# Macaron block on one core: feed-forward results turned in 32 by 32 squares and added onto x by a transfer; the attention numerator added up by transfers, its second product on GpSimd

## The reference

```
x = x + 0.5 * ffn(layernorm(x))        # for each of 8 experts: acc += (silu(x @ wg) * (x @ wu)) @ wd
x = x + attention(layernorm(x))        # linear attention, 16 heads of 8 channels, bias bo
x = x + 0.5 * ffn(layernorm(x))
# attention, along the 1024 positions t of a batch, per head:
#   S_t = S_{t-1} + phi(k_t) v_t^T ;  z_t = z_{t-1} + phi(k_t)
#   out_t = (phi(q_t) S_t) / (phi(q_t) . z_t + eps) ; then @ Wo.T + bo
```

## Time and profile before

| | before |
|---|---|
| device time, median of 3 runs | 2106.57 us (2105.96 to 2108.25) |
| device time of the profiled execution | 2106.5 us |
| span of the profiled execution | 2104.7 us |
| instructions | 29593 |
| PE busy | 99% |
| DVE busy | 86% |
| ACT busy | 67% |
| POOL busy | 22% |
| DMA, mean | 56 GB/s |
| granted TensorE clock | 1.0 throughout |

### The profile page before, as it was taken

The page is one execution under the profiler, slowest core; times in us unless marked ns, Lnnn a source line. Parts: engine busy times, 40 slices in busy tenths (PEclk is TensorE's granted clock), DMA queues, the critical chain, the costliest instruction groups (busy, mean ns, idle before and its releaser), DMA issues.

```text
span 2104.7 us, 29593 instructions
## 1 busy us (share of the span) xinstructions
PE 2075.6 (99%) x9716; PEld 951.7 (45%) x9716; DVE 1800.3 (86%) x3023; ACT 1416.3 (67%) x2466; POOL 459.1 (22%) x370
## 2 busy tenths in 40 slices
PE   8999999999999999999999999999999999999999
PEld 4444444444444444444444444444444444444444
DVE  8877988899889989887989888888998899877776
ACT  6777667766776686668666766677667666666665
POOL 6400122212321321122112311231132213200000
PEclk9999999999999999999999999999999999999999
DMA  7000323122222221312212232041222233100000
GB/s 206 6 11 11 91 66 76 44 68 56 71 61 67 71 56 61 82 26 61 73 45 71 56 81 63 25 96 56 67 56 71 61 76 81 31 7 10 11 11 5
DMA packets 106186, 117.84 MB, mean 56 GB/s; under 512 B 53168, under 2 KB 83504, under 8 KB 106032
## 3 DMA queue, kind: packets, MB, share of 16 engines
q1 hardware_dynamic: 106032, 115.95, 21.6%
HBM read 86.31 MB, written 17.30 MB: 49 GB/s over the span
## 4 chain that ended last, share of the span: by engine, by line
PE 86%; DVE 8%; ACT 3%; issue 3%; DMA 0%; POOL 0%; SPq 0%; ACTq 0%; DVEq 0%
PE bank L545 10%; PE bank L558 9%; PE bank L560 9%; PE bank L559 9%; PE bank L534 9%; PE bank L532 9%; PE bank L533 9%; PE bank L546 9%; PE bank L547 9%; DVE bank L834 3%; DVE h_lo L840 2%; ACT silu_sb L647 1%; DVE arena L948 1%; PE bank L617 1%; PE bank L597 1%
## 5 line engine op out<-in xcount | busy, mean ns | idle before, releaser
L647 ACT ACTIVATE silu_sb<-bank,scal 128x512 f32<-128x512 f32 x1024 | 703.2, 687 | 615.9 <-PE bank L534 611.8
L834 DVE SCALAR_TENSOR_TENSOR bank<-silu_sb,scal,bank 128x512 f32<-128x512 f32 x992 | 745.4, 751 | 283.6 <-ACT silu_sb L647 280.3
L840 DVE TENSOR_TENSOR h_lo<-bank,h_hi 128x512 f16<-128x512 f32 x992 | 674.1, 680 | 0.1
L654 ACT ACTIVATE h_hi<-bank 128x512 f16<-128x512 f32 x992 | 585.4, 590 | 6.3 <-DVE bank L834 5.1
L545 PE MATMUL bank<-xn,wu_hi 128*128 128x512 f16 x1024 | 389.0, 380 | 15.3 <-DVE h_lo L840 12.5
L532 PE MATMUL bank<-xn,wg_hi 128*128 128x512 f16 x1024 | 388.1, 379 | 2.5 <-DVE wg_lo L822 2.5
L558 PE MATMUL bank<-h_hi,wd_lo 128*128 128x512 f16 x1024 | 388.1, 379 | 0.7 <-DVE wd_lo L822 0.7
L546 PE MATMUL bank<-xn,wu_hi 128*128 128x512 f16 x1024 | 388.1, 379 | 0.0
L547 PE MATMUL bank<-xn,wu_lo 128*128 128x512 f16 x1024 | 388.1, 379 | 0.0
L534 PE MATMUL bank<-xn,wg_lo 128*128 128x512 f16 x1024 | 388.1, 379 | 0.0
L533 PE MATMUL bank<-xn,wg_hi 128*128 128x512 f16 x1024 | 388.1, 379 | 0.0
(11 more groups left out here) (126 smaller groups left out, 1343.4 us busy)
## 6 DMA issues: line engine op xcount, KB each, us to landing
arena<-rep_scratch SPq DMA_DIRECT2D x128, 512.0 KB, 7.1
rep_scratch<-arena SPq DMA_DIRECT2D x16, 512.0 KB, 2.6
x_tok<-in_L_attn_x SPq DMA_DIRECT2D x16, 256.0 KB, 5.3
term_scratch<-arena SPq DMA_DIRECT2D x8, 512.0 KB, 3.4
arena<-term_scratch SPq DMA_DIRECT2D x8, 512.0 KB, 3.2
arena<-rden_scratch SPq DMA_DIRECT2D x8, 512.0 KB, 8.6
out<-x_tok SPq DMA_DIRECT2D x16, 256.0 KB, 2.4
arena<-in_L_ffn_Wg SPq DMA_DIRECT2D x4, 512.0 KB, 8.8
```

Of the source, the lines that this page charges most:

```text
L647: act.activation(silu_sb[:, n % 3, :], gate_ps[n % NG][:, :], ACT.Silu, scale=unscale[G[group(n)]]).then_inc(sem("silu"), 1)
L654: act.activation(h_hi[:, n % NH, :], up_ps[n % NUP][:, :] if n >= NC else h_sb(n), ACT.Copy).then_inc(sem("h_hi"), 1)
L834: dve.scalar_tensor_tensor(up_ps[n % NUP][:, :] if n >= NC else h_sb(n), silu_sb[:, n % 3, :], (h_scale if n >= NC else h_first)[group(n)] ...
L840: dve.tensor_tensor(h_lo[:, n % NH, :], up_ps[n % NUP][:, :], h_hi[:, n % NH, :], ALU.subtract).then_inc(sem("h_lo"), 1)
```

## The change

What it does:

- **Segment ends** (32 of 33): VectorE turns `down_sb` in squares of 32 by 32 (`turn`, one instruction 128x512), SP writes the squares to DRAM with four transfers (`turn_out`, 64 KB each, in pieces of 128 B), and GpSimd's queue issues a transfer of 256 KB that adds them onto x (`resid`). The four TensorE transposes and the VectorE addition go. The last end keeps the old way.
- **Low halves of the norms** (`lo`, `att_lo`): VectorE to GpSimd.
- **Rounds**: `q_state` and, at a batch's end, `att_out` move from VectorE to GpSimd. `num_add` is a transfer of 512 KB that adds the ring's buffer onto `num`, issued from GpSimd's queue, 56 of them.
- **VectorE's slot**: `low(n-1)` now stands ahead of the planned steps, not behind them.
- The planner spaces some steps wider (`TURNED` = 8 for 4, projections 3 slots apart for 2, `den_load` and `den` later).

The diff, cut to its core:

```
@@ planner
+TURNED = 8
-        t = vector(t + TT + 1, of + "lo", i, T + 64)
+        t = gpsimd(t + TT + 1, of + "lo", i, 1)
+    def results(t, e):
+        t = vector(t, "turn", e, T + 64)
+        sp_at[t].append(("turn_out", e))
+        pool_at[t + 3].append(("resid", e))
+        return t + 6
-            take(NU_A + LAG + 1, "out_T", 0, "resid")
-        t = take(NC * (s + 1) + LAG + 1, "out_T", s + 1, "resid")
+            results(NU_A + LAG + 1, 0)
+        if s + 1 < NS:
+            t = results(NC * (s + 1) + LAG + 1, s + 1)
+        else:
+            t = take(NC * NS + LAG + 1, "out_T", NS, "resid") + 2
...
-            n = 2 + (d > 1)
-            v = gpsimd(max(v, begin + PACE * d), "k_v", r, n)
+            v = gpsimd(max(v, begin + PACE * d), "k_v", r, 2)
             if d > 1:
-                pool_at[v - n].insert(-1, ("num_add", r - 1))
+                pool_at[v - 2].append(("num_add", r - 1))
...
-            for j in range(BB):
-                v = vector(v, "q_state", BB * r + j, T + 64, True)
-        u = gpsimd(v, "num_add", r, 2)
-        t = max(u + 1, recip)
-        for a in blocks_of(b):
-            t = vector(t, "att_out", a, T + 64, True)
+            v = gpsimd(v, "q_state", r, 2)
+        pool_at[v + 1].append(("num_add", r))
+        u = v + 4
+        t = max(u, recip)
+        t = gpsimd(t, "att_out", b, 2)
@@ sync engine
+                    elif kind == "turn_out":
+                        sp.wait_ge(sem("turn"), i + 1)
+                        for k in range(P // Q32):
+                            sp.dma_start(turn_d[i, :, cols(k, Q32)].rearrange("(s p) n -> p s n", p=Q32),
+                                         turn_sb[cols(k, Q32), :].rearrange("p (s n) -> p s n", n=Q32)
+                                         ).then_inc(sem("turn_out"), 16)
@@ vector engine
             for n in range(FIRST, LAST):
                 if 0 <= n < NU:
                     h(n)
+                if NC <= n - 1 < NU:
+                    low(n - 1)
                 for kind, i in dve_at[n]:
...
+                    elif kind == "turn":
+                        dve.wait_ge(sem("down_evac"), i + 1)
+                        if i:
+                            dve.wait_ge(sem("turn_out"), 16 * (P // Q32) * i)
+                        dve.transpose(turn_sb[:, :], down_sb[:, :]).then_inc(sem("turn"), 1)
...
-                if NC <= n - 1 < NU:
-                    low(n - 1)
@@ gpsimd
+                    elif kind == "resid":
+                        blk = segs[max(i - 1, 0)][1]
+                        pool.wait_ge(sem("turn_out"), 16 * (P // Q32) * (i + 1))
+                        if i:
+                            pool.wait_ge(sem("resid"), 16 * i)
+                        pool.dma_start(x_block(blk), turn_d[i, :, :].rearrange("(t p) e -> p t e", p=P), accum_op=ALU.add
+                                       ).then_inc(sem("resid"), 16)
...
+                    elif kind == "q_state":
+                        b, d = divmod(i, D)
+                        pool.wait_ge(sem(f"q_rep{i % NR}"), 16 * (i // NR + 1))
+                        if d == 0 and b:
+                            pool.wait_ge(sem("wo"), BB * b)
+                        pool.wait_ge(sem("kv_scan"), BB * (i + 1))
+                        for j in range(BB):
+                            state = ring("kv", i)[:, cols(j)]
+                            pool.tensor_tensor(state if d else num[:, cols(j)], ring("q_rep", i)[:, cols(j)], state, ALU.mult
+                                               ).then_inc(sem("q_state"), 1)
+                    elif kind == "att_out":
+                        pool.wait_ge(sem("num_add"), added(i * D + D - 1))
+                        pool.wait_ge(sem("rden_load"), 16 * (i + 1))
...
                     elif kind == "num_add":
                         if i % D > 1:
                             pool.wait_ge(sem("num_add"), added(i - 1))
-                        for j in range(BB):
-                            pool.wait_ge(sem("q_state"), BB * i + j + 1)
-                            pool.tensor_tensor(num[:, cols(j)], num[:, cols(j)], ring("kv", i)[:, cols(j)], ALU.add
-                                               ).then_inc(sem("num_add"), 1)
+                        pool.wait_ge(sem("q_state"), BB * (i + 1))
+                        pool.dma_start(num, ring("kv", i), accum_op=ALU.add).then_inc(sem("num_add"), 16)
```

More of the change, by code:

```diff
@@ L191, in att_head @@
             act_at[t + 1].append(("k_evac", a))
-            t = take(t + 2, "proj_q", a)
+            t = take(t + 3, "proj_q", a)
             act_at[t + 1].append(("q_evac", a))
-            t = take(t + 2, "proj_v", a)
+            t = take(t + 3, "proj_v", a)
             act_at[t + 1].append(("v_evac", a))
@@ L222, in att_rounds @@
         sp_at[t].append(("den_store", b))
-        t = max(t + 2, before)
+        t = max(t + 3, before)
         sp_at[t].append(("den_load", b))
-        recip = vector(vector(t + 3, "den", b, L + 64), "recip", b, 9 * P)
+        recip = vector(vector(t + 6, "den", b, L + 64), "recip", b, 9 * P)
         sp_at[recip].append(("rden_store", b))
@@ L268, in macaron_program @@
         down_in[max(later[n + LAG], max(down_in, default=0))].append(n)
-    consumer = {"norm_T": "lo", "out_T": "resid", "proj_k": "k_evac", "proj_q": "q_evac",
+    consumer = {"norm_T": "lo_first", "out_T": "resid", "proj_k": "k_evac", "proj_q": "q_evac",
                 "proj_v": "v_evac", "wo": "att_resid", "watt_T": "watt_copy",
@@ L658, in down_evac @@
                 if e:
-                    act.wait_ge(sem("out_T"), e)
+                    act.wait_ge(sem("turn"), e)
                 act.wait_ge(sem("out_scale"), min(e + 1, 3))
@@ L971, in _ @@
                         dve.reciprocal(den_all[:, :], den_all[:, :]).then_inc(sem("recip"), 1)
-                    elif kind == "att_out":
-                        b, j = divmod(i, BB)
-                        dve.wait_ge(sem("num_add"), added(b * D + D - 1) - BB + j + 1)
-                        dve.wait_ge(sem("rden_load"), 16 * (b + 1))
-                        dve.tensor_tensor(num[:, cols(j)], num[:, cols(j)], rden[:, cols(j)], ALU.mult
-                                          ).then_inc(sem("att_out"), 1)
                     elif kind == "att_resid":
@@ L1046, in _ @@
                         row_pow(2 + i % 2, "att_var_eps", i + 1, "att_rstd")
+                    elif kind == "lo":
+                        pool.wait_ge(sem("hi"), i + 1)
+                        pool.tensor_tensor(half_tok[:, i % 2, 1, :], xn_tok[:, 0, :], half_tok[:, i % 2, 0, :], ALU.subtract
+                                           ).then_inc(sem("lo"), 1)
+                    elif kind == "att_lo":
+                        pool.wait_ge(sem("att_hi"), i + 1)
+                        pool.tensor_tensor(half_tok[:, 2 + i % 2, 1, :], xn_tok[:, 1, :], half_tok[:, 2 + i % 2, 0, :],
+                                           ALU.subtract).then_inc(sem("att_lo"), 1)
                     elif kind == "x_bias":
@@ L1069, in _ @@
                                                ALU.mult).then_inc(sem("k_v"), 1)
+                    elif kind == "q_state":
[11 more added lines that the diff above has]
+                        pool.wait_ge(sem("rden_load"), 16 * (i + 1))
+                        for j in range(BB):
+                            pool.tensor_tensor(num[:, cols(j)], num[:, cols(j)], rden[:, cols(j)], ALU.mult
+                                               ).then_inc(sem("att_out"), 1)
                     elif kind == "num_add":
```

48 lines of the change are left out of this document (15 added, 33 removed).

## The result

| | before | after |
|---|---|---|
| device time, median | 2106.4 us (4 runs, 2105.96 to 2108.25) | 2084.94 us (4 runs, 2084.9 to 2086.86) |
| ratio | | 0.9897, 95% interval 0.9884 to 0.9911 |
| device time and span of the profiled execution | 2106.5, 2104.7 us | 2084.94, 2083.2 us |
| DVE busy | 86% | 81% |
| POOL busy | 22% | 31% |

The change takes 21.5 us off; 28 were forecast. The time lies inside the range and 7 us above the number.

The account below looks back on a forecast made before the run. TensorE, busy 99% of the span, was taken as the bound, with its waits for VectorE. 2106.5 - 13.8 (transposes) - 16 (waits) + 2 (new waits) = 2078.7, given as 2078 us; range 2066 to 2098.

Parts of the forecast that it names:

- Transposes, 13.8 us: TensorE at segment ends: 32 of 33 `out_T` go, each 0.43 us on the bounding engine, 13.8 us off the path.
- Waits of `up`, 16 us less: TensorE waiting at `up` for VectorE's `low`: 14 us less from the changed order, 2 from projections three slots apart.
- the stretch: The kernel from 200 to 1800 us; its matmuls were weighed at 1573 us, leaving 27 us of waits before the change.
- well under half: Expected sign on TensorE: the waits at `up` come to well under half of those in the wait list before.
- sign of being wrong: The forecast is wrong if `up` still waits 20 us, or if VectorE stands at scans for `k_v`.
- slot account: VectorE's lag summed slot by slot against TensorE's allowance: 19 us of waits before, 5 us for the changed order.
- 2 us for projections spaced wider: Part of the 16 us of waits saved, booked for projections now three slots apart.
- 2 us for new waits: All waits the change adds, blocks 0 and 1 costing 1 to 2 us each; ends 0 and 10.
- The turn: VectorE's turn at segment ends: 0.68 us each, 32 of them, 22 us; its stores and adding transfer hidden elsewhere.
- Rival A: VectorE's scans stand behind GpSimd on the shared way into SBUF, the 16 us are gone: 2093 us; chance 0.15.
- Rival B: TensorE waits at batch ends for the numerator's adding transfer, landing beyond 13.6 us: 2128 us; chance 0.12, with beyond.
- Rival C: Whole kernel: no change by more than 0.2% (4.2 us), needing waits of 24 to 32 us; chance 0.05.

Follow-up runs that it names:

- Run 3: The changed kernel with all 33 segment ends as before (TensorE transposes, VectorE adds onto x, no turn): 2098.5 us, ratio 0.9957.
- run 9: The changed kernel with `exp` planned behind four slots free of other ScalarE steps, and `shift` made by GpSimd: 2074.3 us, ratio 0.9845.
- run 1: The kernel before with only `low(n-1)` put ahead of the planned VectorE steps: 2098.7 us, ratio 0.9959.
- run 2: The changed kernel with `low(n-1)` put back behind the planned VectorE steps: 2091.7 us, ratio 0.9928.
- run 5: The changed kernel with `exp` planned only where the four slots up to it hold no other ScalarE step, ATT_STEP 100 for 102: 2080.2 us, ratio 0.9872.
- run 7: The changed kernel with `shift` made by GpSimd right behind `rstd`, VectorE only negating the mean: 2078.1 us, ratio 0.9861.
- run 10: The changed kernel with only the constant ATT_STEP, the distance at which attention blocks are planned, at 100 for 102: 2086.9 us, ratio 0.9904.

## Why the prediction was right, and where 7 us went

- **Transposes, 13.8 us: right.** Run 3 gives 13.6. That leaves 21.5 - 13.8 = 7.7 us for all else, where 16 - 2 = 14 were booked: this is where the 7 us are. The start distance in the timeline, 0.43 us, was the right measure; the listed 0.60 would have given 19.
- **Waits of `up`, 16 us less: right in kind, too large.** In the stretch 9.3 went; the list of waits says the same, 32.3 us left of 58.4, 55%, where "well under half" was to be seen. The prediction's sign of being wrong was that `up` still waits 20 us. By that list it does, by the measure of the stretch it is 18.0, just inside. What failed is the slot account's silent assumption that `silu` is always in time. It kept a ledger of VectorE alone. Two things of ScalarE were missing. First, `norm` waits in ScalarE's queue for `shift`, a planned step of VectorE, and the change puts those behind `low`: the text said such a step "now only delays the next slot", and forgot who waits for it. Second, `norm` and high halves fall into the short slots ahead of `exp`. Both were in the trace of before, the first as the wait of 39.6 us at `norm`, a row that the prediction did not read, the second as the `norm` steps in the slots ahead of batch 2's `exp`. Freed of both (run 9), the kernel has 9.6 us of waits, near the 27 - 16 = 11 that the prediction booked. Part of that nearness can be chance: the account itself found 19 of the 27 before, and the 2 us for projections spaced wider were not tried alone.
- **Order and load, 14 us together.** The prediction did not part them; the expectations of runs 1 and 2 did, with 11 and 8 us for the order. Measured are 6 to 9 us for the order, 3 for the load under the old order and nothing under the new. So three parts of the change, the low halves, the products and the adding transfers onto `num`, gain nothing that shows once `low` stands first. Whether they would beside the cures of runs 5 and 7 was not tried.
- **2 us for new waits: about right in size, not in place.** `wo` waited once, 1.1 us. In segment 0 TensorE waits for GpSimd's `low`, 4.1 us counted from the weight loads where it was 1.6 before, which was not foreseen; that the new work in GpSimd's queue delays it is likely and was not tried.
- **The turn: 0.702 us against 0.68.** The stores landed in 1.9 us in the median against 4, the adding transfers in 4.6 and 5.6 us, each 11.7 at most, against bounds of 19.8 and 7.1. GpSimd's issue took 0.88 us (onto `num`) and 1.34 us (onto x) against 1. By the Trainium skill (DMA: Bandwidth & Descriptors, Specifications) pieces under 512 B cost a reading and rewriting. No price of it can be read here: 64 KB in pieces of 128 B landed in 1.9 us in the median (11.7 at most), 256 KB of `out` in 2.3, 2.4 before, and TensorE waited for none of it.
- **Busy times.** GpSimd 635.5 us, with issues; 650 was forecast with them, 560 without. VectorE 1691, not 1653: `shift` grew by 11 us, `low` by 4, and the forecast took away whole durations although neighbours overlap by 0.1 us in busy time. With 191 instructions fewer that is 19 us; 4 us stay open.
- **Rival A named the right mechanism and the wrong victim.** It priced scans standing behind GpSimd; their maximum is 1.285 us, as before. The planner keeps GpSimd's steps out of their slots. It does not do so for `shift`, whose two inputs are in SBUF as well: 0.155 us in the median, 1.53 at most. By the Trainium skill (SBUF - State Buffer, Who interferes with whom) VectorE and GpSimd share a pair of ports, and it is an exclusive lock; the trace agrees, `shift` ends at 380.45 where `q_state` ends at 380.43. A small instruction is no safer: this one of 128x4 lost up to 1.37 us, `att_lo` of 128x512 up to 1.00 before.
- **Rival B did not come.** The transfer onto `num` lands in 4.6 us in the median, a third of the 13.6 from which it decides, and in 11.7 at most. `att_out` waited for it five times, up to 10.9 us, and `wo` for `att_out` once, 1.1 us. **Rival C** neither.

## What to carry to other kernels

When an engine's order is changed, look up who waits for each step that moves back, also on engines that are not the bound: a queue that stands for 0.15 us of work holds up everything behind it. A ledger of one engine is right only as long as its inputs are in time; read the wait rows of its suppliers before trusting it. Taking work off an engine pays only where that engine is late: with `low` first, 111 us less on VectorE gained 0.2. And a small step in a chain between engines can cost more than large ones with slack: here `rstd` and `shift` on one engine gained 6.9 us.

## What the runs showed of the hardware that was not expected

- An adding transfer of 512 KB within SBUF landed in 4.6 us in the median (11.7 at most), faster than a copy of 512 KB from DRAM to 128 partitions (7.0), though it also reads where it writes.
- Issuing one from GpSimd's queue is not free: 0.88 us for 128 rows of 1024, 1.34 us for 128x4x128, against 0.37 us for an issue on SP and 0.49 in the median for the stores of the turn.
- VectorE's transpose of 128x512 fp32 in squares of 32 takes 0.697 to 0.704 us, about as long as an addition of that shape (0.684).
- A VectorE instruction on 128x4 with two inputs in SBUF took from 0.15 to 1.53 us; the one shown ended with GpSimd's `q_state`. In run 10 one took 2.26 us.
